# A windowed gather: differences in two instructions per column offset, gather in strips of 32 columns, stores of 32 partitions

## What is computed

```python
def _window_inds(sorted_idx, k=K):
    start = jnp.maximum(0, i - k // 2)
    end = jnp.minimum(N, i + k // 2 + 1)
    pos = jnp.minimum(start[:, None] + jnp.arange(k)[None, :], (end - 1)[:, None])
    return jnp.take(sorted_idx, pos, axis=1)

def _get_graph_features(feats, inds_list, perm, W_lin, b_lin, k=K):
    for inds in inds_list:                       # the four orders
        neigh = gather(feats, inds)
        gf = concatenate([broadcast(center), neigh - center])
    x = stack(per_method)[..., perm]             # channels of 4 orders interleaved
    x16 = x.astype(float16)                      # heads of 32, attention among the K rows
    ...
```

## Time and profile before

| | us |
|---|---|
| median of 3 runs | 3178.42 |
| the profiled execution | 3193.7 |
| its span | 3191.9 |
| gather of layer 1, 304.3 to 594.5 | 290.2 |
| attention and norm of layer 1, 594.5 to 1203.5 | 609.0 |
| gather of layer 2, 1203.5 to 1496.8 | 293.3 |

### The profile page before, as it was taken

One profiled execution on the slowest core, in us unless ns is written; L12 is line 12 of the kernel. 1 busy time (PEld: TensorE's weight loads), 2 busy tenths in 40 slices (PEclk: granted clock), 3 DMA queues, 4 the chain that ended last, 5 costly groups with the idle time before them and its releaser, 6 DMA issues. The chain is left out here.

```text
span 3191.9 us, 101454 instructions
## 1 busy us (share of the span) xinstructions
PE 2304.3 (72%) x37716; PEld 1694.6 (53%) x37716; DVE 2343.3 (73%) x4333; ACT 1750.2 (55%) x3096; POOL 1045.3 (33%) x985
## 2 busy tenths in 40 slices
PE   0122777499999935763999999902979988888867
PEld 0111555488888834443999999801344444444432
DVE  8566899476777748895777777725568988888875
ACT  0575587665666623876888888801434444444432
POOL 0001000366666621001666666600023333333321
PEclk9999888576788867886999999955989999999987
DMA  0774488743434432888333333271122222222210
GB/s 31 157 181 97 109 211 199 179 94 91 94 92 96 95 29 67 198 201 203 86 86 88 90 86 88 65 77 52 52 70 67 73 69 69 66 69 69 63 54 13
DMA packets 395931, 309.43 MB, mean 97 GB/s; under 512 B 147101, under 2 KB 347875, under 8 KB 395744
## 3 DMA queue, kind: packets, MB, share of 16 engines
q1 hardware_dynamic: 395744, 306.68, 39.9%
HBM read 200.96 MB, written 105.62 MB: 96 GB/s over the span
## 5 line engine op out<-in xcount | busy, mean ns | idle before, releaser
L839 PE MATMUL pQ<-QM,QX 128*128 128x64 f16 (+1 forms) x5760 | 753.4, 236 | 0.0
L837 PE MATMUL pQ<-neigh_lo,QX 128*128 128x32 f16 (+1 forms) x5760 | 736.9, 213 | 0.0
L837 PEld LDWEIGHTS pQ<-neigh_lo,QX 128*128 128x128 f16 x5760 | 726.5, 163 | 5.6
L839 PEld LDWEIGHTS pQ<-QM,QX 128*128 128x128 f16 x5760 | 719.2, 160 | 1.6
L929 POOL TENSOR_TENSOR Dm<-Sc,mx 128x450 f32<-128x450 f32 x384 | 366.0, 953 | 301.2 <-DVE mx L891 301.0
L936 POOL TENSOR_TENSOR Ap<-E,R 128x450 f32<-128x450 f32 x384 | 366.7, 955 | 96.6 <-DVE R L904 88.3
L672 ACT ACTIVATE QS<-QT 128x5760 f16<-128x5760 f16 x32 | 345.7, 10803 | 35.1 <-DVE QT L543 29.3
L955 ACT ACTIVATE Sc<-pQ 128x450 f32<-128x450 f32 x384 | 211.4, 551 | 234.8 <-PE pQ L839 228.2
L891 DVE TENSOR_REDUCE mx<-Sc 128x15 f32<-128x450 f32 x384 | 239.2, 623 | 124.4 <-ACT Sc L955 102.5
L654 PE MATMUL pext<-onehot,FX 128*128 128x283 f16 x2048 | 295.8, 313 | 17.3 <-issue 17.3
L1836 POOL TENSOR_TENSOR MT<-cb,decay 128x512 f32 (+1 forms) x128 | 185.3, 1466 | 333.7 <-DVE zero_m L1734 266.8
(11 more groups left out here) (341 smaller groups left out, 4162.9 us busy)
## 6 DMA issues: line engine op xcount, KB each, us to landing
scratch_q<-QT SPq DMA_DIRECT2D x32, 1440.0 KB, 6.0
scratch_r<-QS SPq DMA_DIRECT2D x32, 1440.0 KB, 12.5
QX<-scratch_q SPq DMA_DIRECT2D x768, 60.0 KB, 1.9
QM<-scratch_r SPq DMA_DIRECT2D x192, 240.0 KB, 2.8
hall<-scratch_hi SPq DMA_DIRECT2D x16, 1024.0 KB, 9.5
lall<-scratch_lo SPq DMA_DIRECT2D x16, 1024.0 KB, 14.7
Wg<-in_in_proj SPq DMA_DIRECT2D x64, 256.0 KB, 2.7
Wh<-in_in_proj SPq DMA_DIRECT2D x64, 256.0 KB, 2.8
```

Of the source, the lines that this page charges most:

```text
L837: nc.tensor.matmul(pQ[:, p, u // PB, o + 32:o + BW], qx[u], W["neigh_lo"][:, 0:O], start=False, stop=True, skip_group_check=True)
L839: last = nc.tensor.matmul(pQ[:, p, u // PB, o:o + BW], qx[u], qm[u], start=False, stop=True, skip_group_check=True)
```

## The change

The 128 rows are put in another order: the order of the points (m) is slow, the channel fast (`rep` is tiled). With it the gather by matmul needs no zeros between: FX is gone, t16 and l16 are the weights, in strips of 32 columns that write 32 rows of `pext` each. The cast t16 is made by ACT in place of DVE. `ext` gets ten columns more (EXT 566 becomes 576; the added ones match no rank), so that the first sub-blocks of group 0 can be computed with all others. The differences are two instructions per place n, groups 0 to 10 and the last group, and one at the end that writes the first two sub-blocks of group 0 again, behind a wait for the six before it. Differences come one step after the load in place of two, QS two steps after in place of three, and at the end of ACT's step. QS<-QT copies columns 0 to 29, and GpSimd clears QS once. The scratch keeps its layout, so every store is cut into four, one per m, of 32 partitions each, with every fourth row of the scratch; the counters count 192 per batch in place of 48. The scratch arrays are named anew (q16 becomes x16, r16 becomes q16).

```diff
-EXT = LEAD * K + N + HALF - 1
+EXT = (LEAD + 1) * K + N + HALF - 1
...
-        FX = sb("FX", [128, 2, 2, M * NT * 128], F16)
...
-        QV = 12
+        QV = 2 * PTS + 1
+        QO = 16 * 3 * M
...
-        def window_rows(eng, k, n, sem_):
-
-            last = None
-            for g0, g1, s0, s1 in ((0, 1, 2, SUBS), (1, GROUPS - 1, 0, SUBS),
-                                   (GROUPS - 1, GROUPS, 0, NSUB - SUBS * (GROUPS - 1))):
-                base = 44 + n + GP * g0 + PTS * s0
-                at = ext[:, k, base:base + 1]
-                ctr = cen[:, k, GP * g0 + PTS * s0 + n:GP * g0 + PTS * s0 + n + 1]
-                G, U = g1 - g0, s1 - s0
-                src = bass.AP(at.tensor, at.offset, [at.ap[0], [GP, G], [1, K], [PTS, U]])
-                cbc = bass.AP(ctr.tensor, ctr.offset, [ctr.ap[0], [GP, G], [0, K], [PTS, U]])
-                last = eng.tensor_tensor(QT[:, k, g0:g1, n * K:(n + 1) * K, s0:s1], src, cbc, ALU.subtract)
-                last.then_inc(sem_, 1)
-
-            U = 2 if n < LEAD - PTS else 1
-            at = ext[:, k, K * n:K * n + 1]
-            ctr = cen[:, k, n:n + 1]
-            src = bass.AP(at.tensor, at.offset, [at.ap[0], [1, K], [K * PTS, U]])
-            cbc = bass.AP(ctr.tensor, ctr.offset, [ctr.ap[0], [0, K], [PTS, U]])
-            eng.tensor_tensor(QT[:, k, 0, n * K:(n + 1) * K, 0:U], src, cbc, ALU.subtract).then_inc(sem_, 1)
+        def rows(tile, k, at, *dims):
+
+            first = tile[:, k, at:at + 1]
+            return bass.AP(first.tensor, first.offset, [first.ap[0]] + [list(d) for d in dims])
...
                 if at(3):
-                    (b, _), k = at(3), (k - 3) % 4
+                    (b, _), k = at(3), (k0 - 3) % 4
                     sp.wait_ge(q_v, b * QV + 5 * QV)
-                    sp.dma_start(scratch["q16"][bass.ds(b * GROUPS, GROUPS), :, :].rearrange("g p x -> p g x"),
-                                 QT[:, k, :, :, :].rearrange("p g x s -> p g (x s)")).then_inc(q_out[k], 16)
-                    sp.dma_start(scratch["c16"][bass.ds(b * GROUPS, GROUPS), :, :].rearrange("g p x -> p g x"),
-                                 cen16[:, k, :].rearrange("p (g x) -> p g x", g=GROUPS)).then_inc(q_out[k], 16)
+                    x16 = scratch["x16"][bass.ds(b * GROUPS, GROUPS), :, :].rearrange("g (c m) x -> m c g x", m=M)
+                    c16 = scratch["c16"][bass.ds(b * GROUPS, GROUPS), :, :].rearrange("g (c m) x -> m c g x", m=M)
+                    for m in range(M):
+                        sp.dma_start(x16[m], QT[m * C:(m + 1) * C, k, :, :, :].rearrange("p g x s -> p g (x s)"))\
+                            .then_inc(q_out[k], 16)
+                        sp.dma_start(c16[m], cen16[m * C:(m + 1) * C, k, :].rearrange("p (g x) -> p g x", g=GROUPS))\
+                            .then_inc(q_out[k], 16)
                 if at(4):
-                    (b, _), k4 = at(4), k0 % 4
+                    (b, _), k = at(4), k0 % 4
                     sp.wait_ge(q_turned, b + 1)
-                    sp.dma_start(scratch["r16"][bass.ds(b * GROUPS, GROUPS), :, :].rearrange("g p x -> p g x"),
-                                 qs[:, k4 % 2, :, :, :].rearrange("p g s x -> p g (s x)")).then_inc(q_out[k4], 16)
+                    q16 = scratch["q16"][bass.ds(b * GROUPS, GROUPS), :, :].rearrange("g (c m) x -> m c g x", m=M)
+                    for m in range(M):
+                        sp.dma_start(q16[m], QS[m * C:(m + 1) * C, k % 2, :, :, :].rearrange("p g s x -> p g (s x)"))\
+                            .then_inc(q_out[k], 16)
...
+            nc.gpsimd.memset(QS[:, :, :, :, :].rearrange("p b g s x -> p (b g s x)").bitcast(F32), 0.0).then_inc(zeroed, 1)
+            pool.wait_ge(zeroed, 4)
...
-                    dve.wait_ge(f_used, b + 3)
                     dve.wait_ge(gathered, b + 1)
-                    v.tensor_copy(t16[:, h, :], ptok[:, h, 0:NT * C]).then_inc(t16_ready, 1)
                     dve.wait_ge(t16_ready, b + 1)
                     v.tensor_tensor(l16[:, h, :], ptok[:, h, 0:NT * C], t16[:, h, :],
                                     ALU.subtract).then_inc(l16_ready, 1)
-                    dve.wait_ge(l16_ready, b + 3)
-                    for hl, src in enumerate((t16, l16)):
-                        fx = FX[:, hl, h, 0:1]
-                        dst = bass.AP(fx.tensor, fx.offset, [fx.ap[0], [NT * 128 + 1, M], [M, NT * C]])
-                        v.tensor_copy(dst, src[:, h, :].unsqueeze(1).to_broadcast([128, M, NT * C]))\
-                            .then_inc(fx_ready, 1)
-
...
-                if at(2):
-                    (b, i), k = at(2), (k - 2) % 4
+                if at(1):
+                    (b, i), k = at(1), (k - 1) % 4
...
-                    dve.wait_ge(q_out[k], i * 48 + 48)
+                    dve.wait_ge(q_out[k], i * QO + QO)
                     for n in range(PTS):
-                        window_rows(v, k, n, q_v)
+                        for g0, g1, s1 in ((0, GROUPS - 1, SUBS), (GROUPS - 1, GROUPS, NSUB - SUBS * (GROUPS - 1))):
+                            p0 = GP * g0 + n
+                            v.tensor_tensor(QT[:, k, g0:g1, n * K:(n + 1) * K, 0:s1],
+                                            rows(ext, k, LEAD * K + HALF - 1 + p0, (GP, g1 - g0), (1, K), (PTS, s1)),
+                                            rows(cen, k, p0, (GP, g1 - g0), (0, K), (PTS, s1)),
+                                            ALU.subtract).then_inc(q_v, 1)
+                    dve.wait_ge(q_v, b * QV + 5 * QV - 1)
+                    v.tensor_tensor(QT[:, k, 0, 0:PTS * K, 0:2].rearrange("p (n j) s -> p n j s", n=PTS),
+                                    rows(ext, k, 0, (K, PTS), (1, K), (K * PTS, 2)),
+                                    rows(cen, k, 0, (1, PTS), (0, K), (PTS, 2)), ALU.subtract).then_inc(q_v, 1)
...
-                    pe.wait_ge(fx_ready, b * 2 + 2)
+                    pe.wait_ge(l16_ready, b + 3)
                     pe.wait_ge(hot_ready, b * M * NT + M * NT)
                     pe.wait_ge(ext_ready, b + 1)
                     for e in range(2):
-                        for n in range(2 * M * NT):
-                            hl, mt = n // (M * NT), n % (M * NT)
-                            last = nc.tensor.matmul(pext[:, h, e, 0:H2], FX[:, hl, h, mt * 128:(mt + 1) * 128],
-                                                    onehot[:, h, mt, e * H2:(e + 1) * H2],
-                                                    start=n == 0, stop=n == 2 * M * NT - 1)
+                        for n in range(2 * NT):
+                            half, t = (t16, l16)[n // NT], n % NT
+                            for m in range(M):
+                                last = nc.tensor.matmul(pext[m * C:(m + 1) * C, h, e, 0:H2],
+                                                        half[:, h, t * C:(t + 1) * C],
+                                                        onehot[:, h, m * NT + t, e * H2:(e + 1) * H2],
+                                                        start=n == 0, stop=n == 2 * NT - 1)
...
-            act.wait_ge(zeroed, 2)
+            act.wait_ge(zeroed, 4)
...
-                if at(3):
-                    (b, i), k3 = at(3), (k - 3) % 4
-                    act.wait_ge(q_v, b * QV + 5 * QV)
-                    act.wait_ge(q_out[(k3 + 2) % 4], (i + 1 + k3 // 2) * 48)
-                    nc.scalar.activation(qs[:, k3 % 2, :, :, :], QT[:, k3, :, :, :].rearrange("p g x s -> p g s x"),
-                                         ACT.Copy).then_inc(q_turned, 1)
                 if at(0):
-                    b, i = at(0)
-                    act.wait_ge(q_out[k], i * 48 + 48)
+                    (b, i), h = at(0), k % 2
+                    act.wait_ge(f_used, b + 3)
+                    act.wait_ge(gathered, b + 1)
+                    nc.scalar.activation(t16[:, h, :], ptok[:, h, 0:NT * C], ACT.Copy).then_inc(t16_ready, 1)
+                    act.wait_ge(q_out[k], i * QO + QO)
                     act.wait_ge(q_v, b * QV + QV)
-                    act.wait_ge(f_used, b + 3)
...
+                if at(2):
+                    (b, i), k2 = at(2), (k - 2) % 4
+                    act.wait_ge(q_v, b * QV + 5 * QV)
+                    act.wait_ge(q_out[(k2 + 2) % 4], (i + 1 + k2 // 2) * QO)
+                    nc.scalar.activation(QS[:, k2 % 2, :, :, 0:PTS * K],
+                                         QT[:, k2, :, 0:PTS * K, :].rearrange("p g x s -> p g s x"), ACT.Copy).then_inc(q_turned, 1)
...
-                    src = scratch["q16"][bass.ds(t, 2), :, :].rearrange("g p x -> p g x")
+                    src = scratch["x16"][bass.ds(t, 2), :, :].rearrange("g p x -> p g x")
...
-                    sp.dma_start(QM[:, kq:kq + 2, 0, :], scratch["r16"][bass.ds(t, 2), :, :]
+                    sp.dma_start(QM[:, kq:kq + 2, 0, :], scratch["q16"][bass.ds(t, 2), :, :]
...
-    c["rep"] = np.repeat(np.eye(C, dtype=np.float32), M, axis=1)
```

(41 more changed lines are left out.)

3 lines of the change are left out of this document (2 added, 1 removed).

## The result

| | before | changed |
|---|---|---|
| median of 4 runs | 3178.44 | 3207.48 (3206.52 to 3214.31) |
| ratio | | 1.0091, 95% interval 1.0072 to 1.0111 |
| the profiled execution | 3193.7 | 3206.58 |

The kernel became slower by the mechanism forecast: stores of 32 adjacent partitions run at little more than half the rate of whole ones and set the period of the gather. The loss is 29.0 us where 18.6 were forecast (3197 from 3178.4).

A forecast was written before the change was run, and what follows sets the result against it. Before, DVE (14.2 us a batch) plus a 1.3 us transfer-queue surcharge set the gather's period; after, transfers would: 13.85 + 1.85 + 0.3 = 16.0 us a batch, +9.1 us a gather, +18.3 in all, 3197 us, range 3100 to 3235.

The forecast's parts named there:

- part 4: Gather's stores: pieces of 32 adjacent partitions move at 213 GB/s, so the eight large pieces take 13.85 us a batch.
- The sum: Gather, per batch: large pieces 13.85, c16 1.85, fb 0.3, together 16.0 us of transfers, above DVE and ACT's 12.5 to 13.1.
- part 3: PE's gather matmuls: strips run side by side, 3.6 us in place of about 9; nothing counted as saved.
- Rival (a): Gather's large stores: 32-partition stores are not slowed, period 13.1 us, 3104 us; chance 0.33 with the cases between.
- 1.85 us for c16: Gather's stores of centres: 1.85 us a batch with most of the write trail hidden; bounds 1.2 and 4.7.
- a chance of 0.10 for 3282 us: Rival in the gather's stores: the trail of c16 does not hide, 18.85 us a batch, 3282 us; chance 0.10.
- that order plays no part: Gather's store queue: neither order nor alternation of partition ranges helps, as read from the join's loads; no gain counted.
- DMA share near 1: Sign in the steady gather: DMA engines busy nearly all the time, with a period of 16 us.
- The size: Both gathers: each ends 9.1 us later, +18.3 us in all, giving 3197 us.

The follow-up runs named there:

- cut32: The kernel before, only its three stores a batch each cut into four of 32 adjacent partitions; 1.0190 of before.
- cut128: The kernel before, each store cut into four pieces of all 128 partitions and 3 of the 12 groups; 1.0011 of before.
- stride4: The kernel before, each store cut into four pieces of every fourth partition, 32 partitions each; 0.9957 of before.
- after_whole: The changed kernel with its three stores a batch whole again, 128 partitions each, exchange of rows left out; 3105.66 us, 0.9746 of before.
- after_c_whole: The changed kernel with only the centres (c16) stored whole, exchange of their rows left out, large stores still cut; 1.0022 of before.
- after_0213: The changed kernel with the four pieces of every large store issued in the order 0, 2, 1, 3; 0.9938 of before.
- after_again: The changed kernel timed once more, unedited, on the chip of other runs; 1.0074 of before.
- c_stride: The kernel before, only the centres (c16) stored in four transfers of every fourth partition, large stores whole; 1.0009 of before.

## Why the prediction was right, step by step

**The store rate (part 4), right.** Taken at 213 GB/s from a load in the other direction. Most slices stand at 185 to 235; those of 396 to 476 in which only packets of the large pieces start (63 slices of 0.4 us) have a mean of 198, 7% under what I took. `cut32`, `cut128` and `stride4` show that the place of a piece's partitions does it.

**The sum.** 16.0 us a batch foretold, 16.05 measured in the first gather. DVE 12.5 foretold, 12.75 measured; large difference 2490 against 2520 ns; ACT 12.1 against 11.8; copy 10.2 against 10.24. The first store, foretold 36.2 us after GpSimd's first clearing (341.4 less 305.2), left 36.4 us after it in both gathers. The terms as I gave them add up to 341.1, not 341.4; that moves the forecast by 0.3 us a gather. The last traffic, foretold for 601.4, less the 1.8 us by which the gather began earlier 599.6, ended at 599.3. The order of time at the start shows the chain: clearing of QS, cast, strip matmuls, differences, store.

```profile
316.70 4.90 POOL L565 MEMSET QS<- 128x5760 f32 x1
321.63 0.28 ACT L655 ACTIVATE t<-ptok 128x128 f16<-128x128 f32 x1 [29.28 <-POOL QS L565]
...
331.69 7.76 DVE L598 TENSOR_TENSOR QT<-ext,cen 128x1650 f16<-128x1650 f32 x6 [0.26 <-issue]
...
339.79 0.35 SPq L544 DMA_DIRECT2D scratch_x<-QT  x1
```

**The strips (part 3), right, and worth nothing here.** 16 groups of four start about 0.24 us apart and end 4.0 us after the first begins (3.9 foretold). PE works half as much, and its granted clock in the steady stretch is 0.57 against 0.83 before, nearer the lower of its two levels. It costs nothing: PE waits 9.8 us a batch for fb. In `after_whole`, where DVE bounds, it is 0.58 as well.

**Rival (a), that 32-partition stores are not slowed, priced about right and not the case.** The period without slowed stores was foretold as 13.1 us and the time as 3104, 0.977 of before; `after_whole` took 12.9 (its copies start at 393.67 and, six later, at 471.28) and 0.975.

**The terms inside the sum: two misses that cancel.** I had 1.85 us for c16, up to 4.7 if nothing hid, and a chance of 0.10 for 3282 us. `after_c_whole` shows that even the uncut store costs no more, and that the cut one is no cheaper. The lengths of the packets in the changed kernel's trace size both terms, over six batches from 400 on: per batch the engines are busy 12.9 us with the 960-byte packets of the large pieces (67 ns each), 1.1 with the 90-byte packets of c16 (11 ns each), 0.3 with the rest, and 1.8 us with none. Where only large packets start, the engines' busy share is 0.92 and not 1 either. If these pauses are shared out by busy time, which is an estimate, the large pieces take 14.5 us where I had 13.85 and c16 1.2 where I had 1.85. So 16.0 came out for the right reason, the rate of the large pieces, but its closeness is luck.

**Wrong: that order plays no part.** "Neither the order nor the alternation of partition ranges helped" was read from the join. `after_0213` changes the order alone and gains 1.1 us a batch. In the join 64-partition transfers stand among those of 32, and loads are not stores; it was evidence about the mean there, not that an order could not help. With the order 0, 1, 2, 3 as the change has it the forecast did not depend on this.

**Wrong: DMA share near 1.** It was 0.89, though the transfers set the period; in `after_c_whole`, without small pieces between the large ones, it was 0.97. The share alone did not show the bound; the rate in slices and the held issues of SP did.

**The size.** Foretold +18.3 us from the gathers, measured +20.0 there; medians differ by 29.0, and by 25.4 in `after_again`. Two things are missing. The first gather became 8.4 us longer where 9.1 were foretold, the second 11.7: its period is 16.7 us (1309.03 to 1409.21 from copy to copy, six of them) against 16.05, and before's second gather was slower than its first as well. Why, no run tells. And the profiled execution of before was 15 us over its median, that of the changed kernel 1 us under its own: I carried the difference of one traced execution over to the median unchanged. `cut128` and `c_stride`, whose times are those of before, have gathers of 579.1 and 577.9, so before's 582.6 was probably some 4 us long; against these the changed kernel's loss is 24 us.

## What to carry to other kernels

Before a store is cut to change the order of rows, look where its pieces lie: pieces of 32 adjacent partitions ran at little more than half the rate, pieces of every fourth partition at the full one. If pieces must be adjacent, queue them so that neighbours lie in different halves (here 37.0 us of both gathers). And price what a change saves apart from what it needs to be possible: here half of what the change saves in the gathers (42.5 of 82.8 us) needed no new order of rows, and with it no new stores.

## What was not expected of the hardware

- Pieces of every fourth partition, large and small in turn, move the same bytes in less time of the DMA engines than whole stores: share 0.67 against 0.82.
- In one queue, pieces of different halves as neighbours bring the period from 16.05 to 14.9 us by their order alone, by partial overlap as I read it; from two queues slices reach 349 GB/s.
- A held issue holds the engine that issues: 38.5 us of ACT in seven batches.
- In the two runs with strided large stores the first attention, which reads them, took 615.8 and 619.5 us, beside 605.4 to 613.7 in all others, one profiled execution each. Why was not tried.
- A slowest dimension of 4 leaves a 1440 KB store at 107 GB/s and the DMA share at 0.26.
